# A graph layer with layer norm: first loads in another order, earlier statistics, degrees by one matmul

## The chip, the cores and the metric

The kernel runs on one core of a Trainium2 chip. The metric is device time in microseconds (us). Three runs of the kernel before took 436.0, 438.15 and 438.83 us, median 438.15.

## The reference

`x` is 4096x256 and `adj` 4096x4096, both float32. With N = 4096 rows:

```
h    = relu((x - mean) / sqrt(var + 1e-5))           # per row of x
deg  = sum(adj, axis=1) + 1e-5                       # per row of adj
out  = x + relu((adj / deg) @ h @ Wn.T + bn + h @ Ws.T + bs)
```

## The kernel before, in words

The host lays `adj` out so that a *unit* is a tile of 128 partitions x 2 x 512: two blocks of 128 columns of `adj` (the contraction) against the 512 rows of one of Q = 8 *groups*. A group has U = 16 units, so there are S = 128 units, and the list `order` (lines 33 and 34) interleaves groups 0 and 1 in the first 32 units, while h is still being made; from unit 32 on the groups follow each other. Unit s of group q and index u needs the two row tiles 2u and 2u+1 of h, called *pair* u. There are 16 pairs.

Products are in three terms of a rounded type: every operand is split into a high part (rounded, made by ScalarE) and a low part (the rest, made by VectorE), and hi*hi, hi*lo and lo*hi are added up in PSUM. A unit is therefore, in this order: a load into one of RING = 4 buffers `adj_raw` (SP's queue), `adj_hi` (ScalarE, line 292), `adj_lo` (VectorE, line 434), an addition into `total` for the degrees (VectorE, line 446; the first of a group is a copy, line 443) and 12 matmuls (TensorE, lines 573 to 575). For 14 units of the groups 0 and 1 the addition is instead a second load that adds in memory (`by_dma`, issued by GpSimd, line 239). The load of unit s waits until high part, low part and VectorE's addition of unit s - 4 are done; `adj_hi` and `adj_lo` of unit s wait until TensorE has used unit s - 4.

A pair of h is made by: a load of x (SP), statistics and their aggregation (VectorE, lines 397 and 401), rstd and shift (GpSimd, lines 214 to 225, started at `norm_at[p]`), two activations into `h_row` (ScalarE, line 295, at `make_at[p]`), `h_hi` (ScalarE, line 316, at `split_at[p]`) and `h_lo` (VectorE, line 426). Tiles 0 and 1 go a shorter way, with VectorE scaling (line 410) and the first unit cut into two halves (lines 312, 421, 555).

Each engine runs its own list in order: a loop over s with fixed places for the other work, so whatever waits holds what stands behind it. The lists at lines 45 to 56 are these places, counted in units. After its 16 units a group has: its product split (lines 351 and 469, at `product_at`), its h made again, transposed (line 590) and multiplied with Ws, then weighed with Wn (line 599), joined, activated, added to x and stored.

Degrees: when a group's units are in `total`, VectorE adds its two halves to `sums` (128x512, partition by row; line 458). TensorE then multiplies each of four 128x128 blocks of `sums` with a column of ones (line 623), which puts the degree of 128 rows into one column of a PSUM bank, and VectorE adds 1e-5 and takes the reciprocal (lines 474 and 476). The last group's degrees come directly ahead of unit 127. `weigh_last` and lines 533 to 538 are the tail of the last group: of its four tiles, 0 and 1 go through ScalarE and GpSimd (lines 387 and 283), 2 and 3 through VectorE (line 538).

Of the kernel before, what the change touches and what calls it, by code (L numbers as in the profile page):

```python
# [5 lines left out]
P = 128  # L6
# [9 lines left out]
RING = 4  # L16
# [5 lines left out]
def gnn_layer(nc, x, adj, wn, ws, bn, bs, out):  # L22
# [27 lines left out]
    product_at = [32, 42, 52] + [last_unit[q] + 3 for q in range(3, Q)]  # L50

    norm_at = [0, 0, 2, 3] + [2 * p - 4 for p in range(4, PAIRS)]

    make_at = [0, 1, 3] + [2 * p - 2 for p in range(3, PAIRS - 1)] + [2 * PAIRS - 5]
    split_at = [0, 1, 3] + [2 * p - 1 for p in range(3, PAIRS - 1)] + [2 * PAIRS - 4]
    sums_at = [38, 45, 54, 64] + last_unit[4:]

    with ExitStack() as ctx:
# [24 lines left out]
        ones = sb("ones", [P, 1])  # L83
# [8 lines left out]
        deg = sb("deg", [P, 2, UI])  # L92
# [17 lines left out]
        s_ones = sem("ones_ready")  # L110
# [50 lines left out]
        def _(sp):  # L161
# [19 lines left out]
            sp.dma_start(adj_raw[:, 0, 0, :], adj[0, 0, :, 0, :]).then_inc(s_raw0, 16)  # L181
            sp.dma_start(adj_raw[:, 0, 1, :], adj[0, 0, :, 1, :]).then_inc(s_raw[0], 16)
# [5 lines left out]
            for s in range(RING, S):  # L188
                load_unit(s)
                if s % 2 == 0 and s // 2 + 2 < PAIRS:  # L190
                    load_x(s // 2 + 2)
# [17 lines left out]
        def _(pool):  # L209
# [32 lines left out]

            def add_bias(q):
                pool.wait_ge(s_owned, q + 1)
                if q == 0:
                    pool.wait_ge(s_bsum, 1)
                nc.gpsimd.tensor_tensor(own[:, :, :], own[:, :, :], b_sum[:, :, :].broadcast_to([P, UI, F]), ALU.add) \  # L247
                  .then_inc(s_ownb, 1)
# [17 lines left out]
            nc.gpsimd.memset(ones[:, :], 1.0).then_inc(s_ones, 1)  # L266
            for s in range(S):
                for p in range(1, PAIRS):
                    if s == norm_at[p]:
                        norm(p)  # L270
                for n in range(len(by_dma)):
# [8 lines left out]
            for t in range(2):  # L280
                row = (Q - 1) * UI + t
                pool.wait_ge(s_relu, Q + t)
                nc.gpsimd.tensor_tensor(x_sb[:, row, :], x_sb[:, row, :], own[:, t, :], ALU.add).then_inc(s_tail[t], 1)

        @block.scalar
        def _(act):
# [70 lines left out]
            nc.scalar.dma_start(x_sb[:, 1, :], x[:, 1, :]).then_inc(s_x1, 16)  # L357
            nc.scalar.dma_start(x_sb[:, 2:4, :], x[:, 2:4, :]).then_inc(s_x[1], 16)
# [26 lines left out]
            for t in range(2):  # L385
                act.wait_ge(s_last, t + 1)
                nc.scalar.activation(own[:, t, :], own[:, t, :], ACT.Relu).then_inc(s_relu, 1)
# [6 lines left out]
        def _(dve):  # L394
# [54 lines left out]
            def join_sums(q):  # L449
                dve.wait_ge(s_add, vector_added[last_unit[q]])  # L450
                if q < 2:
# [3 lines left out]
                    dve.wait_ge(s_both, q + 1)  # L455
                if q >= 1:
                    dve.wait_ge(s_summed, q)
                nc.vector.tensor_tensor(sums[:, :], total[:, q % 3, 0, :], total[:, q % 3, 1, :], ALU.add).then_inc(s_sums, 1)
# [41 lines left out]
            split_unit(1)  # L500
            for s in range(2, S):
# [3 lines left out]
                for p in range(2, PAIRS):  # L505
# [29 lines left out]
            for t in range(2, UI):  # L535
# [6 lines left out]
        def _(pe):  # L542
# [37 lines left out]
            def turn(q):  # L580
# [5 lines left out]
                if q >= 1:  # L586
                    pe.wait_ge(s_deg, q)
# [26 lines left out]
            def sum_degrees(q):  # L614

                pe.wait_ge(s_sums, q + 1)
                pe.wait_ge(s_htlo, 2 * q + 2)
                if q == 0:
                    pe.wait_ge(s_ones, 1)
                else:  # L620
                    pe.wait_ge(s_deg, q)
                for t in range(UI):
# [76 lines left out]
```

## Time and profile before

| | |
|---|---|
| median of 3 runs | 438.15 us |
| the profiled execution | 436.03 us, span 434.0 us |
| TensorE | 419.2 us busy, 97% of the span, granted clock 0.995 on average |
| VectorE | 360.0 us, 83% |
| ScalarE | 208.0 us, 48% |
| GpSimd | 113.7 us, 26% |
| DMA | 83.98 MB, 194 GB/s on average |

Busy time of TensorE counts matmuls from start to a modelled end, and they overlap: a 512-column matmul is given 0.39 us, while the next one starts after 0.23. So its busy share says little about lost time; the starts do. In the timeline a row gives start, duration, engine, line, operation, out<-in, shape and count; in square brackets stands the idle time ahead of it and what ended that. PE is TensorE, DVE VectorE, ACT ScalarE, POOL GpSimd, SP SyncE; a q behind the name is the engine's issuing queue.

### The profile page before, as it was taken

The page shows a single profiled execution, that of the slowest core. Times are in us where ns is not written, and L with a number is a line of the kernel's source. Part 1 is how long each engine was busy: PE and PEld are TensorE (multiplying, and loading weights), DVE is VectorE, ACT ScalarE, POOL GpSimd, SP SyncE. Part 2 cuts the span into 40 slices and gives each one's busy share as a digit, 9 for nine tenths or more (in the row PEclk, how much of TensorE's full clock was granted, in tenths as well). Part 3 has the DMA queues.
Part 4 walks back from the last instruction along what each step waited for, and adds up shares of the span by engine and source line. Part 5 has one row for each costly group of instructions (what it writes and reads, how often), then busy time and mean ns, then how long its engine had stood idle before and what let it go on. Part 6 is the DMA issues. An engine that isn't in the chain of part 4 may idle for free.

```text
span 434.0 us, 5622 instructions
## 1 busy us (share of the span) xinstructions
PE 419.2 (97%) x2057; PEld 350.7 (81%) x2057; DVE 360.0 (83%) x421; ACT 208.0 (48%) x267; POOL 113.7 (26%) x107
## 2 busy tenths in 40 slices
PE   7799999988999999999999999999999999999995
PEld 4578877766888888888888888888888888888884
DVE  5688888989899896996797796979878897869934
ACT  4675555556533733734442544435342643426411
POOL 4365676741020303432203202002110302003021
PEclk9989999999999999999999999999999999999999
DMA  8779999999945474465347364545745465453501
GB/s 281 250 236 316 310 308 287 290 233 287 272 152 195 145 231 158 142 225 166 109 136 239 127 209 154 192 145 160 242 141 194 138 205 183 146 194 101 189 2 48
DMA packets 25482, 83.98 MB, mean 194 GB/s; under 512 B 2800, under 2 KB 4336, under 8 KB 25456
## 3 DMA queue, kind: packets, MB, share of 16 engines
q1 hardware_dynamic: 22864, 75.64, 52.0%
q0 software_dynamic: 2016, 7.34, 8.3%
q10 hardware_dynamic: 576, 0.66, 0.5%
q8 instruction: 16, 0.26, 0.3%
q14 instruction: 10, 0.08, 0.1%
HBM read 79.43 MB, written 4.19 MB: 193 GB/s over the span
## 4 chain that ended last, share of the span: by engine, by line
PE 74%; DVE 8%; POOL 8%; ACT 4%; issue 3%; DMA 3%; DVEq 0%; POOLq 0%; ACTq 0%; SPq 0%
PE banks L573 20%; PE banks L574 20%; PE banks L575 20%; PE banks L599 10%; DVE adj_lo L434 3%; POOL rstd L216 3%; POOL shift L225 2%; ACT adj_hi L292 2%; DMA adj_raw<-adj_in 2%; POOL rstd L214 2%; DVE total L446 2%; PE banks L590 2%; PE banks L623 1%; ACT h_row L295 1%; DVE stats L397 1%
## 5 line engine op out<-in xcount | busy, mean ns | idle before, releaser
L573 PE MATMUL banks<-adj_hi,h_hi 128*128 128x512 f32 x508 | 201.5, 397 | 7.6 <-DVE adj_lo L434 6.0
L292 ACT ACTIVATE adj_hi<-adj_raw 128x1024 fp32r<-128x1024 f32 x127 | 133.9, 1057 | 146.9 <-PE banks L575 128.2
L575 PE MATMUL banks<-adj_lo,h_hi 128*128 128x512 f32 x508 | 198.6, 391 | 0.0
L574 PE MATMUL banks<-adj_hi,h_lo 128*128 128x512 f32 x508 | 198.6, 391 | 0.0
L434 DVE TENSOR_TENSOR adj_lo<-adj_raw,adj_hi 128x1024 fp32r<-128x1024 f32 x127 | 167.4, 1318 | 35.4 <-ACT adj_hi L292 34.9
L446 DVE TENSOR_TENSOR total<-total,adj_raw 128x1024 f32<-128x1024 f32 x106 | 131.1, 1237 | 0.0
L573 PEld LDWEIGHTS banks<-adj_hi,h_hi 128*128 128x128 f32 x508 | 95.8, 189 | 31.5 <-issue 10.5
L575 PEld LDWEIGHTS banks<-adj_lo,h_hi 128*128 128x128 f32 x508 | 95.7, 188 | 20.6
L574 PEld LDWEIGHTS banks<-adj_hi,h_lo 128*128 128x128 f32 x508 | 95.9, 189 | 18.4
L253 POOL TENSOR_TENSOR x_sb<-x_sb,own 128x1024 f32<-128x1024 f32 x7 | 29.1, 4161 | 135.3 <-ACT own L355 135.3
L247 POOL TENSOR_TENSOR own<-own,b_sum 128x1024 f32<-128x1024 f32 x8 | 22.6, 2823 | 116.8 <-ACT own L340 116.8
L295 ACT ACTIVATE h_row<-x_sb,shift,rstd 128x256 f32<-128x256 f32 x62 | 32.9, 591 | 32.0 <-POOL shift L222 32.0
L474 DVE TENSOR_SCALAR deg<-banks 128x4 f32<-128x4 f32 x8 | 1.3, 162 | 22.0 <-PE banks L623 22.0
L351 ACT ACTIVATE p_hi<-banks 128x512 fp32r<-128x512 f32 x16 | 9.2, 597 | 20.3 <-PE banks L575 14.1
L599 PE MATMUL banks<-w_hi,ht_lo 128*128 128x256 f32 x64 | 18.1, 283 | 0.0
L599 PE MATMUL banks<-w_lo,ht_hi 128*128 128x256 f32 x64 | 18.1, 283 | 0.0
L599 PE MATMUL banks<-w_hi,ht_hi 128*128 128x256 f32 x64 | 18.1, 282 | 0.0
L216 POOL TENSOR_TENSOR rstd<-rstd,consts 128x2 f32<-128x2 f32 (+1 forms) x17 | 17.3, 1017 | 1.3
L214 POOL TENSOR_TENSOR rstd<-mv,consts 128x2 f32<-128x2 f32 (+1 forms) x17 | 10.5, 617 | 27.2 <-DVE mv L401 27.2
L239 POOL DMA_DIRECT2D total_dma<-adj_in x12 | 10.7, 891 | 22.0 <-PE banks L575 17.7
L599 PE MATMUL banks<-w_hi,p_lo 128*128 128x256 f32 x56 | 15.8, 283 | 0.0
L599 PE MATMUL banks<-w_lo,p_hi 128*128 128x256 f32 x56 | 15.8, 283 | 0.0
(65 smaller groups left out, 288.0 us busy)
## 6 DMA issues: line engine op xcount, KB each, us to landing
adj_raw<-adj_in SPq DMA_DIRECT2D x127, 512.0 KB, 4.0
total_dma<-adj_in POOLq DMA_DIRECT2D x14, 512.0 KB, 7.9
x_sb<-x_in SPq DMA_DIRECT2D x14, 256.0 KB, 6.0
rows_out<-x_sb SPq DMA_DIRECT2D x7, 512.0 KB, 5.0
adj_raw<-adj_in SPq DMA_DIRECT2D x2, 256.0 KB, 4.5
x_sb<-x_in ACTq DMA_DIRECT2D x1, 256.0 KB, 4.2
w_raw<-w_neigh SPq DMA_DIRECT2D x1, 256.0 KB, 5.4
w_raw<-w_self SPq DMA_DIRECT2D x1, 256.0 KB, 6.1
```

What stands on the lines that cost most here:

```text
L214: nc.gpsimd.tensor_tensor(rstd[:, cols], mv[:, cols, 1], consts[:, 0, 0:n], ALU.add).then_inc(s_rstd, 1)
L216: nc.gpsimd.tensor_tensor(rstd[:, cols], rstd[:, cols], consts[:, 1, 0:n], ALU.pow).then_inc(s_rstd, 1)
L247: nc.gpsimd.tensor_tensor(own[:, :, :], own[:, :, :], b_sum[:, :, :].broadcast_to([P, UI, F]), ALU.add) \
L253: nc.gpsimd.tensor_tensor(x_sb[:, rows, :], x_sb[:, rows, :], own[:, :, :], ALU.add).then_inc(s_final, 1)
L292: nc.scalar.activation(adj_hi[:, r, :, :], adj_raw[:, r, :, :], ACT.Copy).then_inc(s_hi, 1)
L295: return nc.scalar.activation(slot, x_sb[:, t, :], ACT.Relu, bias=shift[:, t:t + 1], scale=rstd[:, t:t + 1])
L434: nc.vector.tensor_tensor(adj_lo[:, r, :, :], adj_raw[:, r, :, :], adj_hi[:, r, :, :].bitcast(F32), ALU.subtract).then_inc(s_lo, 1)
L446: nc.vector.tensor_tensor(total[:, q % 3, :, :], total[:, q % 3, :, :], adj_raw[:, s % RING, :, :], ALU.add).then_inc(s_add, 1)
L573: nc.tensor.matmul(bank, h_hi[:, j, feats], adj_hi[:, r, a, :], start=first, stop=False)
L574: nc.tensor.matmul(bank, h_lo[:, j, feats], adj_hi[:, r, a, :], start=False, stop=False)
L575: done = nc.tensor.matmul(bank, h_hi[:, j, feats], adj_lo[:, r, a, :], start=False, stop=last)
L599: last = nc.tensor.matmul(bank, m[:, k, cols], w[:, k, which, :], start=(n == 0), stop=(n == len(terms) - 1))
```

## The change

Loads: all first loads go out on SP, in the order x tile 0, first half of unit 0, x tile 1, x pair 1, second half of unit 0, then as before; x pairs 4 and 5 follow unit 4, and later pairs come one pair earlier. VectorE's start is reordered, and it splits unit 2 ahead of pair 1's h_lo; ScalarE splits unit 2 ahead of making pair 1. The statistics of pairs 4 and up and their scale and shift come one unit earlier. Product 0 is split one unit earlier. Degrees: `sums` is transposed in blocks of 32x32 and each stretch of 32 is added up, which leaves 128x16 partial sums; one matmul with a 0/1 matrix `fold` (1 where two partitions are equal modulo 32) adds the four stretches of 32 partitions; VectorE picks each row's column with a mask and adds. `fold` is made by GpSimd at unit 30. Of the last group's tiles, tile 1 goes through VectorE as 2 and 3 do.

```diff
-    product_at = [32, 42, 52] + ...
+    product_at = [31, 42, 52] + ...
-    norm_at = [0, 0, 2, 3] + [2 * p - 4 for p in range(4, PAIRS)]
+    norm_at = [0, 0, 1, 2] + [2 * p - 5 for p in range(4, PAIRS)]
-    make_at = [0, 1, 3] + ...
-    split_at = [0, 1, 3] + ...
+    make_at = [0, 2, 3] + ...
+    split_at = [0, 2, 3] + ...
...
             sp.dma_start(x_sb[:, 0, :], x[:, 0, :]).then_inc(s_x[0], 16)
             sp.dma_start(adj_raw[:, 0, 0, :], adj[0, 0, :, 0, :]).then_inc(s_raw0, 16)
+            sp.dma_start(x_sb[:, 1, :], x[:, 1, :]).then_inc(s_x1, 16)
+            load_x(1)
             sp.dma_start(adj_raw[:, 0, 1, :], adj[0, 0, :, 1, :]).then_inc(s_raw[0], 16)
...
                 load_unit(s)
-                if s % 2 == 0 and s // 2 + 2 < PAIRS:
-                    load_x(s // 2 + 2)
+                if s == RING:
+                    load_x(4)
+                    load_x(5)
+                if s > RING and s % 2 == 0 and s // 2 + 3 < PAIRS:
+                    load_x(s // 2 + 3)
...
+            def make_fold():
+                nc.gpsimd.memset(fold[:, :], 0.0).then_inc(s_fold, 1)
+                for n, d in enumerate(range(-96, 128, 32)):
+                    pool.wait_ge(s_fold, n + 1)
+                    nc.gpsimd.affine_select(out=fold[:, :], in_=fold[:, :], compare_op=ALU.not_equal, fill=1.0,
+                                            base=d, pattern=[[-1, P]], channel_multiplier=1).then_inc(s_fold, 1)
...
-            nc.gpsimd.memset(ones[:, :], 1.0).then_inc(s_ones, 1)
...
+                if s == 30:
+                    make_fold()
...
-            nc.scalar.dma_start(x_sb[:, 1, :], x[:, 1, :]).then_inc(s_x1, 16)
-            nc.scalar.dma_start(x_sb[:, 2:4, :], x[:, 2:4, :]).then_inc(s_x[1], 16)
...
+                nc.vector.tensor_tensor(sums[:, :], total[:, q % 3, 0, :], total[:, q % 3, 1, :], ALU.add).then_inc(s_sums, 1)
+                dve.wait_ge(s_sums, q + 1)
+                nc.vector.transpose(total[:, q % 3, 0, :], sums[:, :]).then_inc(s_flipped, 1)
+                dve.wait_ge(s_flipped, q + 1)
                 if q >= 1:
                     dve.wait_ge(s_summed, q)
-                nc.vector.tensor_tensor(sums[:, :], total[:, q % 3, 0, :], total[:, q % 3, 1, :], ALU.add).then_inc(s_sums, 1)
+                nc.vector.tensor_reduce(part[:, :], total[:, q % 3, 0, :].rearrange("p (c s) -> p c s", s=32), AX.X, ALU.add) \
+                  .then_inc(s_part, 1)
...
             def degrees(q):
                 dve.wait_ge(s_summed, q + 1)
-                nc.vector.tensor_scalar(deg[:, 0, :], banks[:, SUMMED, 0:UI], DEG_EPS, None, ALU.add).then_inc(s_deg, 1)
-                dve.wait_ge(s_deg, q + 1)
+                if q == 0:
+                    dve.wait_ge(s_quarter, 5)
+                nc.vector.tensor_tensor(picked[:, :, :], banks[:, SUMMED, 0:R // 32].rearrange("p (t n) -> p t n", n=4),
+                                        in_quarter[:, :, :], ALU.mult).then_inc(s_deg, 1)
+                dve.wait_ge(s_deg, 3 * q + 1)
+                nc.vector.tensor_reduce(deg[:, 2, :], picked[:, :, :], AX.X, ALU.add).then_inc(s_deg, 1)
+                dve.wait_ge(s_deg, 3 * q + 2)
+                nc.vector.tensor_scalar(deg[:, 0, :], deg[:, 2, :], DEG_EPS, None, ALU.add).then_inc(s_deg, 1)
+                dve.wait_ge(s_deg, 3 * q + 3)
                 nc.vector.reciprocal(deg[:, 1, :], deg[:, 0, :]).then_inc(s_rdeg, 1)
...
+            nc.vector.memset(in_quarter[:, :, :], 0.0).then_inc(s_quarter, 1)
+            dve.wait_ge(s_quarter, 1)
+            for n in range(4):
+                nc.vector.memset(in_quarter[32 * n:32 * n + 32, :, n], 1.0).then_inc(s_quarter, 1)
             dve.wait_ge(s_x[0], 16)
             statistics((0,), 1)
+            first_scaled(0)
             dve.wait_ge(s_x1, 16)
             statistics((1,), 2)
-            first_scaled(0)
             first_half_unit(0)
-            first_scaled(1)
             first_low(0)
             pair_statistics(1)
+            first_scaled(1)
+            first_half_unit(1)
             first_low(1)
-            first_half_unit(1)
             split_unit(1)
-            for s in range(2, S):
+            pair_statistics(2)
+            split_unit(2)
+            split_h(1)
+            pair_statistics(3)
+            for s in range(3, S):
...
-                for p in range(2, PAIRS):
+                for p in range(4, PAIRS):
                     if s == norm_at[p]:
                         pair_statistics(p)
...
             def sum_degrees(q):
-                pe.wait_ge(s_sums, q + 1)
+                pe.wait_ge(s_part, q + 1)
                 pe.wait_ge(s_htlo, 2 * q + 2)
...
-                for t in range(UI):
-                    last = nc.tensor.matmul(banks[:, SUMMED, t:t + 1], sums[:, t * P:(t + 1) * P], ones[:, :],
-                                            start=True, stop=True)
-                last.then_inc(s_summed, 1)
+                nc.tensor.matmul(banks[:, SUMMED, 0:R // 32], fold[:, :], part[:, :], start=True, stop=True) \
+                  .then_inc(s_summed, 1)
```

## Rows read from the trace of the kernel before

**Rows 1.** Chain that ended last, shares of the span by engine.

```profile
PE 74%; DVE 8%; POOL 8%; ACT 4%; issue 3%; DMA 3%; DVEq 0%; POOLq 0%; ACTq 0%; SPq 0%
```

**Rows 2.** Busy time by stretch; then TensorE's granted clock, DMA share, GB/s.

```profile
core 0: us, PE busy (x) PEld busy (x) DVE busy (x) ACT busy (x) POOL busy (x), PEclk, DMA share, GB/s
8.00:12.00 4.00, 3.32 (x14) 2.15 (x13) 2.29 (x5) 2.25 (x4) 2.28 (x4) 1.00 1.04 409
24.00:28.00 4.00, 4.00 (x14) 3.20 (x13) 3.69 (x7) 1.31 (x3) 3.47 (x4) 0.68 0.79 236
54.00:107.00 53.00, 49.00 (x207) 37.59 (x206) 47.15 (x67) 31.27 (x46) 30.36 (x35) 1.00 1.01 283
285.50:336.70 51.20, 51.20 (x258) 43.52 (x257) 43.47 (x43) 23.05 (x27) 5.82 (x2) 1.00 0.52 174
```

**Rows 3.** Timeline of TensorE: first matmuls of units 1, 2, 4, 5, 15, 32.

```profile
10.50 0.47 PE L573 MATMUL banks<-adj_hi,h_hi 128*128 128x512 f32 x1 [0.19 <-DVE adj_lo L434]
...
14.89 0.47 PE L573 MATMUL banks<-adj_hi,h_hi 128*128 128x512 f32 x1 [1.43 <-DVE adj_lo L434]
...
22.53 0.47 PE L573 MATMUL banks<-adj_hi,h_hi 128*128 128x512 f32 x1 [1.95 <-DVE adj_lo L434]
...
26.95 0.40 PE L573 MATMUL banks<-adj_hi,h_hi 128*128 128x512 f32 x1
...
54.16 0.45 PE L573 MATMUL banks<-adj_hi,h_hi 128*128 128x512 f32 x1
...
106.73 0.50 PE L573 MATMUL banks<-adj_hi,h_hi 128*128 128x512 f32 x1 [1.60 <-DVE p_lo L469]
```

**Rows 4.** Timeline of all engines, the first 13 us.

```profile
1.65 0.42 SPq L182 DMA_DIRECT2D adj_raw<-adj_in  x1
...
5.54 0.41 DVE L410 TENSOR_SCALAR h_row<-x_sb,mv,rstd 128x256 f32<-128x256 f32 x1 [0.50 <-POOL rstd L216]
...
6.70 0.64 ACT L312 ACTIVATE adj_hi<-adj_raw 128x512 fp32r<-128x512 f32 x1 [0.29 <-DMA adj_raw<-adj_in]
...
7.13 0.75 DVE L397 BATCH_NORM_STATS2 stats<-x_sb 128x6 f32<-128x256 f32 x2
7.23 0.29 POOL L264 TENSOR_SCALAR_AFFINE_SELECT ident<-ident 128x128 f32<-128x128 f32 x1
7.24 0.41 ACT L308 ACTIVATE h_hi<-h_row 128x256 fp32r<-128x256 f32 x1
...
7.91 0.25 DVE L401 BATCH_NORM_AGGREGATE mv<-stats 128x2 f32<-128x6 f32 x2
...
8.04 1.06 ACT L292 ACTIVATE adj_hi<-adj_raw 128x1024 fp32r<-128x1024 f32 x1 [0.39 <-DMA adj_raw<-adj_in]
...
9.13 1.23 DVE L434 TENSOR_TENSOR adj_lo<-adj_raw,adj_hi 128x1024 fp32r<-128x1024 f32 x1
...
10.78 1.09 ACT L295 ACTIVATE h_row<-x_sb,shift,rstd 128x256 f32<-128x256 f32 x2 [1.69 <-POOL shift L222]
...
11.91 0.63 ACT L316 ACTIVATE h_hi<-h_row 128x512 fp32r<-128x512 f32 x1
...
12.57 0.69 DVE L426 TENSOR_TENSOR h_lo<-h_row,h_hi 128x512 fp32r<-128x512 f32 x1 [2.22 <-ACT h_hi L316]
```

**Rows 5.** All waits of ScalarE from 54 to 94 us: total, times, longest.

```profile
ACT h_row L295 <- POOL shift L222: 15.5, 7, 3.5
```

**Rows 6.** Timeline of TensorE: one degree sum and the next unit's first matmul.

```profile
285.64 0.94 PE L623 MATMUL banks<-ones,sums 128*128 128x1 f32 x8
286.44 0.49 PE L573 MATMUL banks<-adj_hi,h_hi 128*128 128x512 f32 x1
```

**Rows 7.** DMA queues, 54 to 94 us: packets, MB, share of 16 engines.

```profile
q1 hardware_dynamic: 2640, 8.29, 59.1%
q0 software_dynamic: 864, 3.15, 41.4%
```

**Rows 8.** Timeline of VectorE: its first operation on the last group's degrees.

```profile
423.66 0.16 DVE L474 TENSOR_SCALAR deg<-banks 128x4 f32<-128x4 f32 x1 [7.60 <-PE banks L623]
```

More of the change, by code:

```diff
@@ L48, in gnn_layer @@
     degrees_at = [w + 1 for w in weigh_at[:-1]]
-    product_at = [32, 42, 52] + [last_unit[q] + 3 for q in range(3, Q)]
-    norm_at = [0, 0, 2, 3] + [2 * p - 4 for p in range(4, PAIRS)]
-    make_at = [0, 1, 3] + [2 * p - 2 for p in range(3, PAIRS - 1)] + [2 * PAIRS - 5]
-    split_at = [0, 1, 3] + [2 * p - 1 for p in range(3, PAIRS - 1)] + [2 * PAIRS - 4]
+    product_at = [31, 42, 52] + [last_unit[q] + 3 for q in range(3, Q)]
+    norm_at = [0, 0, 1, 2] + [2 * p - 5 for p in range(4, PAIRS)]
+    make_at = [0, 2, 3] + [2 * p - 2 for p in range(3, PAIRS - 1)] + [2 * PAIRS - 5]
+    split_at = [0, 2, 3] + [2 * p - 1 for p in range(3, PAIRS - 1)] + [2 * PAIRS - 4]
     sums_at = [38, 45, 54, 64] + last_unit[4:]
@@ L82, in gnn_layer @@
         sums = sb("sums", [P, R])
-        ones = sb("ones", [P, 1])
+        fold = sb("fold", [P, P])
+        in_quarter = sb("in_quarter", [P, UI, 4])
+        part = sb("part", [P, R // 32])
+        picked = sb("picked", [P, UI, 4])
         ident = sb("ident", [P, P])
@@ L91, in gnn_layer @@
         consts = sb("consts", [P, 3, 2])
-        deg = sb("deg", [P, 2, UI])
+        deg = sb("deg", [P, 3, UI])
         banks = ctx.enter_context(nc.psum_tensor("banks", [P, 8, 512], F32))
@@ L109, in gnn_layer @@
         s_ident = sem("ident_ready")
-        s_ones = sem("ones_ready")
+        s_fold = sem("fold_step_done")
+        s_quarter = sem("in_quarter_ready")
+        s_flipped = sem("sums_flipped")
+        s_part = sem("part_sums_ready")
         s_consts = sem("consts_ready")
@@ L279, in _ @@
             add_bias(Q - 1)
[L280 to L283, printed above, removed]
+            row = (Q - 1) * UI
+            pool.wait_ge(s_relu, Q)
+            nc.gpsimd.tensor_tensor(x_sb[:, row, :], x_sb[:, row, :], own[:, 0, :], ALU.add).then_inc(s_tail[0], 1)
         @block.scalar
@@ L384, in _ @@
             product_high(Q - 1)
-            for t in range(2):
-                act.wait_ge(s_last, t + 1)
-                nc.scalar.activation(own[:, t, :], own[:, t, :], ACT.Relu).then_inc(s_relu, 1)
+            act.wait_ge(s_last, 1)
+            nc.scalar.activation(own[:, 0, :], own[:, 0, :], ACT.Relu).then_inc(s_relu, 1)
             for b in range(2, UI):
@@ L534, in _ @@
                                                in1=own[:, t, :], op0=ALU.mult, op1=ALU.add).then_inc(s_last, 1)
-            for t in range(2, UI):
+            for t in range(1, UI):
                 row = (Q - 1) * UI + t
@@ L586, in turn @@
                 if q >= 1:
-                    pe.wait_ge(s_deg, q)
+                    pe.wait_ge(s_deg, 3 * q)
                 for k in range(KC):
@@ L614, in sum_degrees @@
             def sum_degrees(q):
-                pe.wait_ge(s_sums, q + 1)
+                pe.wait_ge(s_part, q + 1)
                 pe.wait_ge(s_htlo, 2 * q + 2)
                 if q == 0:
-                    pe.wait_ge(s_ones, 1)
+                    pe.wait_ge(s_fold, 8)
                 else:
-                    pe.wait_ge(s_deg, q)
-                for t in range(UI):
-                    last = nc.tensor.matmul(banks[:, SUMMED, t:t + 1], sums[:, t * P:(t + 1) * P], ones[:, :],
-                                            start=True, stop=True)
-                last.then_inc(s_summed, 1)
+                    pe.wait_ge(s_deg, 3 * q)
+                nc.tensor.matmul(banks[:, SUMMED, 0:R // 32], fold[:, :], part[:, :], start=True, stop=True) \
+                  .then_inc(s_summed, 1)
             def weigh(q):
```

## The prediction, made before the change was run

> **What bounds it now.** I read the chain of waits first: 74% of it is TensorE [rows 1], so the question is when TensorE is not fed. Busy time doesn't say, because the ends of matmuls are modelled; the starts of the units do (a unit is 12 matmuls of 512 columns). From unit 5 to unit 15 a unit takes (54.16 - 26.95)/10 = 2.72 us [rows 3]; that is TensorE's own pace. Unit 1 to unit 5 takes 16.45 us where four units need 10.88, and unit 15 to unit 32 takes 52.57 where 17 need 46.25. So 5.6 us are lost at the start and 6.3 us between units 15 and 32. In the stretch of a later group of rows TensorE is busy for all of its 51.20 us [rows 2], and a microsecond there can only be won by taking work off TensorE.
>
> Of the 5.6 us, 1.7 are a clock loss: unit 4 runs from 22.53 to 26.95, 4.42 us, and the granted clock of 24 to 28 us is 0.68 on average, so part of it at the lower of the two levels (1.2 of 2.4 GHz), behind a gap of 1.95 us [rows 2, 3]. The rest are gaps on adj_lo of units 2 and 4. In the first rows VectorE waits 2.22 us for h_hi before it goes on to unit 2, and ScalarE waited 1.69 us for the shift before it made that h [rows 4]: an in-order queue stands behind a chain of statistics. Most of the 6.3 us has the same cause: all of ScalarE's waits between 54 and 94 us, 15.5 us in 7, are for GpSimd's shift, none is for a load [rows 5].
>
> **The change, part by part.** *First loads.* Tile 1 and pair 1 go from ScalarE's queue to SP's, two issues of some 0.42 us [rows 4], so everything behind them on SP is issued up to 0.9 us later. The second half of unit 0 is taken on landing at 6.70 and unit 1 at 8.04 [rows 4]; in the order below they are needed at 9.0 and 9.45, so I cost the delay at nothing. ScalarE loses two issues ahead of a wait; nothing comes of that either. Five small memsets on VectorE lie ahead of its first load.
>
> *The start, walked through.* VectorE scales tile 0 until 5.95 as before. The statistics of tile 1 now come behind that (one of the pair's, 0.4 + 0.2), so the low half of unit 0 ends near 7.3, h_lo near 7.6, then pair 1's statistics (7.13 to 8.16 before, 1.03) end at 8.6, tile 1 is scaled by 9.0 (0.41), ScalarE's h_hi of it is there at 9.45 (0.41) and only then does ScalarE split unit 1, until 10.5 (1.06); VectorE's part ends at 11.75 (1.23). TensorE starts unit 1 at 11.8, **1.3 us later** than 10.50 [rows 3, 4]. From there the new order pays. ScalarE splits unit 2 by 11.55 without waiting for h; the shift of pair 1 is there at 8.6 + 2.6 = 11.2 (8.16 to 10.78 before), h is made by 12.65 and h_hi by 13.3 (1.09, 0.63). VectorE: pair 2's statistics to 12.7, unit 2 to 13.9, h_lo to 14.5 (0.69). Unit 2 starts at 14.55 and no longer at 14.89. Then pair 3's statistics to 15.5, unit 3 to 16.7 (TensorE wants it at 17.3), pair 4's to 17.7, the copy to 18.3, h_lo to 19.0, unit 4 to 20.2; ScalarE waits for shift 2 until 12.7 + 2.6 = 15.3 and has unit 4 split at 18.1. Unit 4 starts at 20.2, 2.3 us earlier. With no gap ahead of it that is longer than 0.3 us I take full clock: another 1.7. **Unit 5 starts 4.0 us earlier, at 22.9.** Bounds: 5.6, all that is lost there now, and 0.
>
> *Statistics with more lead.* From pair 4 on they move one unit ahead, and the x loads of SP with them (one pair ahead, no new wait in front). That is 2.7 us more for GpSimd's chain. ScalarE's 15.5 us in 7 waits are 2.2 each, so they vanish but for the longest. What is late next? VectorE: four units cost it six operations of 128x1024 (four splits, two additions) at the split's 1.23, two h_lo of 0.69 and two statistics of 1.03, 10.8 by these rows where TensorE needs 10.88; the measured busy share between 54 and 107 us, 47.15 of 53, is 9.7 per 10.88 [rows 2, 4]. It keeps ahead, narrowly. Low part of product 0 one unit earlier: unit 32 waited 1.60 us for it [rows 3]; now it stands behind unit 31 on ScalarE and VectorE, whose queues wait for TensorE to finish unit 29, two units before unit 32, and p_hi and the split of unit 32 need 0.63 + 1.06 + 1.23 = 2.9 us after that, by the rows of that size [rows 4]: covered by 5.4. So units 15 to 32 go at 2.72 and **6.3 us** are won; unit 32 starts at 96.4, not 106.73, 10.3 us earlier. Bounds: 6.3 and, if only another wait takes the place, 0.
>
> *Degrees.* Now each group of rows issues 4 matmuls, 8 records, in 0.80 us between its first and the next unit's [rows 6]. One matmul of 16 columns is 2 records of the same weights, 0.2 us at the same 0.1 each; at most 0.46, twice the 0.23 of a 512-column matmul. 0.6 saved (0.34 at least) eight times, seven of them and the last in dense TensorE time: **4.8 us** (2.7 to 4.8). In exchange VectorE gets, per group, a transpose and a reduction of 128x512 and two operations on 128x16. No row shows them. Nearest is h_lo, 128x512 from two operands, at 0.69 [rows 4]; bounds 0.34 (half of it) and, for the farthest row, twice the split of 1024 elements, 2.5. I take 0.69 each and 0.2 for each small one (one of 128x4 took 0.16 [rows 8]), 1.8 in all. In a group of 51.2 us VectorE is busy for 43.5 [rows 2], so 7.7 are free; and behind the last sums it waited 7.60 us for TensorE's matmul [rows 8]. Cost on the path nothing; were that cover gone, 1.8 eight times, 14 us.
> The Trainium skill speaks against the reduction (VectorE: DVE Perf Modes, Rules for kernel authors: tensor_reduce only runs in the slowest mode and should be kept off a hot path). By that rule too the sum is unchanged as long as VectorE isn't the bound; no row here shows a reduction.
>
> *Rest.* The fold matrix is eight GpSimd operations in place of one memset; one such select took 0.29 [rows 4]; I allow up to five times that, 2 to 11 us, once, at a point where GpSimd has only additions by DMA behind it, which are needed 20 us later. The last tile 1 goes from ScalarE and GpSimd to VectorE, one operation of 128x256 (0.41 as [rows 4] have such) ahead of tiles 2 and 3: 0, between -0.4 and +0.5.
>
> **Sum.** 4.0 + 6.3 + 4.8 = 15.1 us. The profiled execution was 436.03, so it would be 420.9; the median of the runs, 438.15, stands 2.1 above it, which gives **423**.
>
> **Rivals.** *The ring of loads becomes the bound (3 in 10).* The DMA engines' share is 1.01 from 54 to 107 us [rows 2]. From 54 to 94 SP's queue took 59.1% of 40 us for 8.29 MB, 2.85 us per MB, and the adding queue 41.4% for 3.15 MB, 5.26 per MB [rows 7]. Four units are 2.62 MB of units and x and, at one added by DMA per 2.5 units, 0.84 of additions: 11.9 us, 2.97 a unit, where TensorE wants 2.72. If these are real occupancy, units 12 to 32 go from 42.0 to 101.4, less a lead of 2: 7.3 + 4.8 won, **426**; if the old pace of units 15 to 32 stays outright, 4.0 + 4.8 won, **429.3**. For it speaks the share; against it, that ScalarE waits for no load there [rows 5] and that 8 to 12 us shows 409 GB/s at a share of 1.04 [rows 2], so a share near one isn't a ceiling of bytes.
> The Trainium skill (DMA: Bandwidth & Descriptors, Where 436 GB/s comes from) puts the HBM side of a core at some 358 GB/s. Four units need 3.46 MB in 10.88 us, 318 GB/s, which that rule allows, and by it alone this rival would have 1 in 10; the 409 measured here is above its figure.
>
> *The clock falls in the new first gaps (1 in 10).* TensorE now idles for over 1 us ahead of the second half of unit 0 and ahead of unit 1. If one or two units then run as unit 4 does now, 1.7 to 3.4 us are lost again, 2.5 in the middle: **425.5**. Against it: there were gaps there before, at full clock.
>
> *The degrees don't get cheaper (1 in 20)*, because the matmul of 128x16 costs as much as the four: **427.8**.
>
> *Slower: VectorE becomes the bound of every group (3 in 100).* Place: the sums ahead of each degree matmul. Price: beyond 7.7 us of added VectorE time in a group, TensorE waits for the excess, eight times. To end 4.4 us above 438 it takes 10.3 + 4.4 of excess, 1.8 a group, so a transpose and a reduction of over 4.5 us each, nearly seven times the row taken: **443** and more.
>
> **Numbers.** My forecast has 5 in 10, 419.5 to 425 by its own bounds. Range 419.5 to 429.5: the low end is the sum with a start that wins all of 5.6 and the runs near the profiled execution, the high end is the ring at its old pace. About 1% is what a measurement of this kernel can tell from no change, 433.8 to 442.5. Faster than that: forecast, ring, clock and degrees, 0.88; same 0.08, two of the rivals together; slower 0.04.
>
> **What would show it.** Unit 1 starting near 11.8, unit 2 near 14.5, unit 4 near 20 at full clock; no wait of ScalarE for the shift beyond 1 us after pair 4; unit 32 near 96 to 97; two records per degree matmul and 0.2 us; VectorE idle still above 5 us per group. I am wrong if ScalarE's waits turn to waits for adj_raw between 30 and 95 us, if the granted clock drops below 1 between 8 and 20 us, or if TensorE waits on the partial sums.

## The result, and the profile after

The changed kernel takes **430.67 us** (median) beside 438.1 for the kernel before: a ratio of 0.9848, 95% interval 0.981 to 0.9886. The gain is 1.5%, about half of what I forecast. One of the four runs of the changed kernel took 2355.36 us; it is left out of the ratio, and why it was so long is not known. The profiled execution is 430.28 us with a span of 428.5; before it was 436.03 and 434.0, so 5.5 us of span have to be placed.

The rows of after, in the order of the rows of before. First TensorE's timeline, at the first matmuls of units 1, 2, 4, 5, 15, 32 [rows 3] and, new, of unit 46 (start, duration, engine and line, operation; in brackets the idle time ahead and what ended it):

```profile
11.88 0.77 PE L610 MATMUL banks<-adj_hi,h_hi 128*128 128x512 f32 x1
...
15.20 0.39 PE L610 MATMUL banks<-adj_hi,h_hi 128*128 128x512 f32 x1
...
20.66 0.47 PE L610 MATMUL banks<-adj_hi,h_hi 128*128 128x512 f32 x1
...
23.48 0.39 PE L610 MATMUL banks<-adj_hi,h_hi 128*128 128x512 f32 x1
...
53.70 0.58 PE L610 MATMUL banks<-adj_hi,h_hi 128*128 128x512 f32 x1 [2.86 <-DVE adj_lo L450]
...
104.90 0.47 PE L610 MATMUL banks<-adj_hi,h_hi 128*128 128x512 f32 x1 [0.47 <-DVE adj_lo L450]
...
152.79 0.50 PE L610 MATMUL banks<-adj_hi,h_hi 128*128 128x512 f32 x1 [1.57 <-DVE adj_lo L450]
```

Unit 5 starts 3.47 us earlier than before. At unit 15 almost all of that is gone (53.70 for 54.16): TensorE stood 2.86 us in front of it, at a place where it had not waited before. By unit 32 the lead is 1.83. From unit 5 to unit 32 TensorE takes 81.42 us where 79.78 were needed before; units 5 to 15 lose 3.0 of these, units 15 to 32 win 1.4 (51.20 for 52.57).

The same starts for every kernel of this study, in us, from TensorE's timeline of each (27 units at 2.72 would be 73.4 from unit 5 to 32). The medians were not all taken side by side: the kernel before took 438.1 us beside after and 435.8 to 436.0 beside the others, so whole kernels are to be compared by their ratios to before:

| kernel | unit 5 | unit 5 to 32 | unit 32 to 127 | unit 45 to 46 | span | median |
|---|---|---|---|---|---|---|
| before | 26.95 | 79.78 | 316.76 | 2.72 | 434.0 | 438.1 |
| after | 23.48 | 81.42 | 313.06 | 4.45 | 428.5 | 430.67 |
| after, no adding loads | 22.27 | 73.44 | 310.99 | 2.72 | 417.2 | 419.41 |
| after, adding loads made plain | 23.65 | 74.65 | 312.02 | 3.59 | 420.8 | 422.09 |
| after, statistics at old places | 23.31 | 80.50 | 313.19 | 4.43 | 427.5 | 428.85 |
| before, no adding loads | 25.44 | 80.36 | 316.81 | 2.72 | 433.1 | 435.24 |
| before, degrees part alone | 27.24 | 78.78 | 312.53 | 3.78 | 429.0 | 431.13 |
| after, w and b earlier | 23.45 | 77.25 | 314.04 | 4.44 | 425.2 | 426.71 |
| after, x in fours | 22.80 | 81.26 | 312.86 | 4.13 | 427.4 | 428.36 |
| after, fold later | 23.42 | 81.64 | 312.69 | 3.97 | 428.3 | 429.7 |
| after, three fixes | 23.16 | 76.85 | 311.30 | 2.72 | 421.8 | 425.11 |
| three fixes, sparser adding | 22.73 | 75.04 | 312.29 | 2.72 | 420.5 | 422.59 |
| the same, x in fours | 23.38 | 75.82 | 311.69 | 2.72 | 421.4 | 423.9 |
| sparser adding, old places | 23.40 | 81.33 | 311.67 | 2.72 | 426.9 | 428.81 |

Behind unit 127 all of them take 10.5 us. Kernels with the new start differ by 1.4 us at unit 5 and those with the old one by 1.8, which is the scatter of that figure.

Next the windows of after, against [rows 2]: the first stretch of the start, the end of the start, units 15 to 32, one late group from degree matmul to degree matmul, and the 2 us behind the new gap (busy time and count of each engine, granted clock, DMA share, GB/s):

```profile
core 0: us, PE busy (x) PEld busy (x) DVE busy (x) ACT busy (x) POOL busy (x), PEclk, DMA share, GB/s
8.00:12.00 4.00, 2.73 (x7) 1.72 (x7) 2.55 (x5) 3.28 (x5) 0.83 (x3) 0.69 1.03 401
24.00:28.00 4.00, 4.00 (x19) 3.31 (x18) 3.97 (x7) 3.51 (x6) 3.41 (x6) 1.00 1.03 324
54.00:107.00 53.00, 50.88 (x213) 40.52 (x212) 48.46 (x67) 32.73 (x46) 34.79 (x41) 0.97 0.93 256
283.10:333.55 50.45, 50.45 (x254) 42.84 (x252) 44.83 (x47) 22.94 (x27) 8.32 (x2) 1.00 0.53 179
54.00:56.00 2.00, 2.00 (x6) 1.53 (x5) 1.97 (x5) 2.00 (x4) 1.34 (x2) 0.50 0.30 119
```

The clock loss of 24 to 28 us is gone, but there are two new ones: from 8 to 12 us the granted clock is 0.69 on average, behind the 1.82 us for which TensorE waited ahead of the second half of unit 0, and from 54 to 56 it is 0.50, which is the 1.2 GHz level, behind the gap at unit 15. Unit 15 takes 4.41 us for that and not 2.72. The late group is 50.45 us long where it was 51.20.

ScalarE's waits, 54 to 94 us [rows 5] and then 24 to 108 (line waited for: total, times, longest):

```profile
ACT adj_hi L311 <- DMA adj_raw<-adj_in: 10.8, 7, 3.1
ACT h_row L314 <- POOL shift L233: 3.4, 3, 1.7
```

```profile
ACT adj_hi L311 <- DMA adj_raw<-adj_in: 29.0, 15, 4.0
ACT h_row L314 <- POOL shift L233: 3.8, 4, 1.7
```

The kernel before shows for 24 to 108 us:

```profile
ACT h_row L295 <- POOL shift L222: 26.3, 10, 4.6
ACT adj_hi L292 <- DMA adj_raw<-adj_in: 7.8, 4, 3.1
```

The two lines have changed places. The waits for the shift are nearly gone, as forecast (26.3 us became 3.8), and nearly as many microseconds of waits for the next unit's load stand where they were. The chain of waits of after names the same thing ahead of unit 15 (start, duration, what):

```profile
38.72 12.51 DMA adj_raw<-adj_in
...
51.25 1.06 ACT adj_hi L311
...
52.33 1.22 DVE adj_lo L450
```

It is a load of 512 KB that took 12.51 us to land. Of after's three unit loads issued between 38 and 44 us the trace gives the first row, of before's two between 38 and 46 the second (shortest, median, longest):

```profile
DMA to landing us min/median/max: 10.6/11.3/12.5
```

```profile
DMA to landing us min/median/max: 7.2/7.4/7.6
```

With four buffers in the ring a load has 4 x 2.72 = 10.9 us, less the two splits of the unit that must leave the buffer (1.06 and 1.23): by this estimate what takes over some 8.6 us comes late, or 7.4 where VectorE also adds that unit (1.22). The two queues, 54 to 94 us [rows 7]:

```profile
q1 hardware_dynamic: 2321, 7.55, 54.1%
q0 software_dynamic: 711, 2.61, 34.6%
```

The degrees: one sum and the next unit's first matmul [rows 6], VectorE's first operation on the last degrees [rows 8], and VectorE's work ahead of unit 46's split:

```profile
282.95 0.29 PE L659 MATMUL banks<-part,fold 128*128 128x16 f32 x2
283.08 0.48 PE L610 MATMUL banks<-adj_hi,h_hi 128*128 128x512 f32 x1
```

```profile
418.15 0.17 DVE L498 TENSOR_TENSOR picked<-banks,in_quarter 128x16 f32<-128x16 f32 x1 [5.25 <-PE banks L659]
```

```profile
148.20 1.21 DVE L469 TENSOR_TENSOR total<-total,total_dma 128x1024 f32<-128x1024 f32 x1
149.44 0.69 DVE L472 TENSOR_TENSOR sums<-total 128x512 f32<-128x512 f32 x1
150.17 0.71 DVE L475 STREAM_TRANSPOSE total<-sums 128x512 f32<-128x512 f32 x1
150.92 0.69 DVE L479 TENSOR_REDUCE part<-total 128x16 f32<-128x512 f32 x1
151.52 1.22 DVE L450 TENSOR_TENSOR adj_lo<-adj_raw,adj_hi 128x1024 fp32r<-128x1024 f32 x1
```

The next unit now starts 0.13 us behind the degree matmul, not 0.80. The transpose and the reduction stand in VectorE's queue straight ahead of adj_lo of unit 46, and unit 46 comes 1.7 us late. How late depends on VectorE's lead, the time from the start of unit 45's split on VectorE to its first matmul: the lead is 2.8 us here, 3.4 in before with the degrees part alone, 3.6 with plain loads and 4.5 without adding loads, and unit 46 is 1.73, 1.06, 0.87 and 0 late, each time what the lead lacks of 4.5.

The chain's shares against [rows 1]; DMA has gone from 3% to 8%:

```profile
PE 71%; DVE 12%; DMA 8%; ACT 3%; issue 2%; POOL 2%; SPq 1%; DVEq 0%; ACTq 0%; POOLq 0%
```

**Where the 5.5 us come from.** Start +3.47, units 5 to 32 -1.64, eight degree sums +5.4 (0.66 to 0.68 each), units 46 and 47 -1.9: together 5.3, the rest is scattered. The start's part is not firm: of before's loss there, 1.7 us are the clock loss at unit 4, and the kernel before without its adding loads, whose start is the same, has none in its trace (granted clock 1.00 from 24 to 28 us behind a gap of 1.66) and starts unit 5 at 25.44, not 26.95.

### The profile page after: what moved, and what is told of

Its sections match the earlier page's. It is cut to its first block, busy times and chain, and to the rows that moved or that the text cites. A ratio compares the mean times of both kernels' runs of the same rounds, so it can differ in the third digit from the quotient of the medians.

```text
span 428.5 us, 5577 instructions
## 1 busy us (share of the span) xinstructions
PE 414.2 (97%) x2009; PEld 347.0 (81%) x2009; DVE 377.5 (88%) x459; ACT 207.6 (48%) x266; POOL 128.8 (30%) x113
## 4 chain that ended last, share of the span: by engine, by line
PE 71%; DVE 12%; DMA 8%; ACT 3%; issue 2%; POOL 2%; SPq 1%; DVEq 0%; ACTq 0%; POOLq 0%
PE banks L610 20%; PE banks L611 20%; PE banks L612 20%; PE banks L636 10%; DMA adj_raw<-adj_in 8%; DVE adj_lo L450 5%; DVE total L462 3%; ACT adj_hi L311 2%; PE banks L627 1%; DVE stats L413 1%; ACT h_row L314 1%; POOL rstd L227 1%; POOL shift L233 1%; PE banks L678 0%; DVE p_lo L491 0%
## 5 line engine op out<-in xcount | busy, mean ns | idle before, releaser
L272 POOL TENSOR_TENSOR x_sb<-x_sb,own 128x1024 f32<-128x1024 f32 x7 | 30.6, 4375 | 127.5 <-ACT own L374 127.5
L266 POOL TENSOR_TENSOR own<-own,b_sum 128x1024 f32<-128x1024 f32 x8 | 31.7, 3961 | 111.2 <-ACT own L359 111.2
L227 POOL TENSOR_TENSOR rstd<-rstd,consts 128x2 f32<-128x2 f32 (+1 forms) x17 | 18.4, 1080 | 1.3
L636 PE MATMUL banks<-w_hi,p_hi 128*128 128x256 f32 x56 | 15.8, 282 | 0.0
```

Source lines behind the costliest of these rows:

```text
L227: nc.gpsimd.tensor_tensor(rstd[:, cols], rstd[:, cols], consts[:, 1, 0:n], ALU.pow).then_inc(s_rstd, 1)
L272: nc.gpsimd.tensor_tensor(x_sb[:, rows, :], x_sb[:, rows, :], own[:, :, :], ALU.add).then_inc(s_final, 1)
L636: last = nc.tensor.matmul(bank, m[:, k, cols], w[:, k, which, :], start=(n == 0), stop=(n == len(terms) - 1))
```

## Experiments

My theory after the result: the loads that add into `total_dma` hold up the unit loads of SP's queue until the ring is empty, and this was hidden before because TensorE was already waiting for late statistics. Rivals: the bytes alone are too many; the x loads with small packets are at fault; the earlier statistics are of no use here; VectorE's added work is the bound.

### Is it the adding loads, and is it their bytes or the adding?

**No adding loads** (the 12 units that they add are missing from the degrees; the first two loads, which only store, stay):

```diff
-                    pool.dma_start(total_dma[:, q, :, :], adj[q, u, :, :, :], accum_op=ALU.add).then_inc(s_dadd[q], 16)
+                    (for n >= 2: nothing)
```

> The changed kernel without the 12 loads that add in memory (units of groups 0 and 1 are then missing from their degrees). Theory A, the adding loads slow SP's queue until the ring of loads runs dry: no gap at unit 15, unit 5 to unit 32 in 73.4 to 75 us instead of 81.4, ScalarE's waits for adj_raw between 24 and 108 us under 5 us instead of 28.9, the whole some 7 us faster than the changed kernel, 423 to 424. Theory B, the statistics between split and addition of every fourth unit hold the loads back: nothing of that changes, the gap at unit 15 stays, 430 to 431. Theory C, the small loads of w and b at units 9 to 13 fill the queue: the gap at unit 15 shrinks to about half, the rest up to unit 32 stays, 428 to 429.

Measured: 419.41 us, ratio 0.9629 (0.9593 to 0.9664). From unit 5 to 32 TensorE takes 73.44, its own pace to the hundredth. ScalarE from 24 to 108 us now waits mostly for TensorE to free a buffer:

```profile
ACT adj_hi L309 <- PE banks L610: 15.6, 14, 1.7
ACT adj_hi L309 <- DMA adj_raw<-adj_in: 7.0, 4, 2.1
```

By the spans the adding loads cost the changed kernel 11.3 us, by the ratios 9.5. 8.0 of them lie between units 5 and 32 and 2.1 behind unit 32, as unit 46 isn't late either; the other 1.2 lie ahead of unit 5, where no adding load has been issued (the first goes out at 37.29 in after), and are scatter.

**The same loads, plain** (each only stores; same bytes, same points of issue; each replaces what was there, so the degrees lack the units loaded ahead of it):

```diff
-  pool.dma_start(total_dma[...], adj[q, u, ...], accum_op=ALU.add)
+  pool.dma_start(total_dma[...], adj[q, u, ...])
```

> The changed kernel with the 12 adding loads turned into plain loads of the same bytes over the same tile, at the same places (the sums of groups 0 and 1 are then those of one unit). If the adding is what slows SP's queue (it needs a read of the destination and a write), the loads land in 5 to 7 us instead of 8 to 10, the gap at unit 15 is gone and unit 5 to 32 takes 75 to 77 us: some 5 us faster than the changed kernel. If it is only the bytes, nothing changes: the gap at unit 15 stays and 81 us.

Measured: 422.09 us, ratio 0.9687 (0.9662 to 0.9711), 74.65 from unit 5 to 32. The DMA issues from 54 to 94 us, first of this kernel, then of after (form, count, KB, median us to landing):

```profile
adj_raw<-adj_in SPq DMA_DIRECT2D x15, 512.0 KB, 5.8
total_dma<-adj_in POOLq DMA_DIRECT2D x8, 512.0 KB, 6.3
```

```profile
adj_raw<-adj_in SPq DMA_DIRECT2D x14, 512.0 KB, 7.8
total_dma<-adj_in POOLq DMA_DIRECT2D x6, 512.0 KB, 8.5
```

With the same bytes all landings are 2 us shorter, and 6.8 of the 8.0 us come back between units 5 and 32. So it is the adding, and only 1.2 the bytes. What in the adding slows the other loads was not tried. The Trainium skill (DMA: Bandwidth & Descriptors, Where 436 GB/s comes from) has some 358 GB/s of the HBM side bind such loads. The traces don't show that as the limit here: with the additions the queues are full at less (from 36 to 54 us the share is 1.02 at 305 GB/s), and 8 to 12 us goes above it at 401 [rows 2 had 409].

### What are the earlier statistics worth?

**After, statistics and x loads at their old places:**

```diff
-    norm_at = [0, 0, 1, 2] + [2 * p - 5 for p in range(4, PAIRS)]
+    norm_at = [0, 0, 1, 2] + [2 * p - 4 for p in range(4, PAIRS)]
...
-                if s == RING: load_x(4); load_x(5)
-                if s > RING and s % 2 == 0 and s // 2 + 3 < PAIRS: load_x(s // 2 + 3)
+                if s % 2 == 0 and s // 2 + 2 < PAIRS: load_x(s // 2 + 2)
```

> The changed kernel with the statistics from pair 4 on and the x loads back at the places of before; start and degrees stay changed. Theory A: loads still late between 35 and 50 us, the gap at unit 15 stays within 1 us, unit 5 to 32 at 80 to 82 us, total 430 to 431. Theory B: the gap at unit 15 goes, ScalarE waits for the shift again, 15 us between 54 and 94, unit 5 to 32 at 79 to 80, total 427 to 428.

Measured: 428.85 us, ratio 0.9846 (0.9823 to 0.987), so no slower than after. ScalarE's two lines (24 to 108 us) change places once more, and the gap at unit 15 is gone although the adding loads, w and b are where they were:

```profile
ACT h_row L311 <- POOL shift L230: 24.0, 9, 4.6
ACT adj_hi L308 <- DMA adj_raw<-adj_in: 9.9, 4, 4.5
```

In this kernel the step that I had priced at 6.3 us is worth nothing or a little less.

**Before, without its adding loads** (the same 12 units missing):

> The kernel before without its 12 adding loads (the first two, which only store, stay; those 12 units are missing from the degrees). Question: how much of what the kernel before loses between units 15 and 32 (6.3 us) came from the late statistics, which was the reason given in the prediction, and how much from the adding loads. Theory (statistics: all of ScalarE's waits there were for GpSimd's shift): units 15 to 32 still take 51 us or more, the kernel 434 to 436. Rival (the adding loads also slow the x loads on which the statistics stand, and those unit loads that nobody was seen to wait for): units 15 to 32 take 46.3 to 48 us and the kernel 429 to 432.

Measured: 435.24 us, ratio 0.9969 (0.9943 to 0.9995). Units 15 to 32 take 51.9 us, and ScalarE still waits for the shift, 26.4 us in 7 from 24 to 108 us:

```profile
ACT h_row L293 <- POOL shift L222: 26.4, 7, 4.6
ACT adj_hi L290 <- DMA adj_raw<-adj_in: 5.3, 5, 1.9
```

So my reading of the kernel before was right: its loss there came from the statistics. Without the additions it gains 0.7 us (1.4 by the ratio); in after the same edit gains 9.5 by the ratio. And yet the additions slow the loads here too: the unit loads issued from 54 to 94 us landed in a median of 5.8 us with them and 3.3 without. They were hidden behind the late statistics.

**Sparser adding loads, statistics at old places** (the best kernel, told below, with the edit of the first experiment of this group):

> The kernel with the three fixes and sparser adding loads, with the statistics and x loads from pair 4 on back at the places of before. Where the loads no longer run dry, this is what the earlier statistics are worth. Theory (the prediction's step: late shifts cost TensorE time): units 5 to 32 take 4 us longer than with the early ones, ScalarE again waits over 15 us for the shift, and the kernel takes 426 to 427. Rival (the shift was only late because the x loads came late on a queue that the adding loads held up): within 1 us of 422.6.

Measured: 428.81 us, ratio 0.9821 (0.9773 to 0.9868), by the medians 6.2 us more than the same kernel with early statistics (422.59), by the ratios 5.2. Units 5 to 32 take 81.33 for 75.04. 1.7 of these 6.3 us are a clock loss behind a late unit (unit 28 takes 4.39 us); ScalarE's waits:

```profile
ACT h_row L311 <- POOL shift L230: 28.5, 9, 4.6
...
ACT adj_hi L308 <- DMA adj_raw<-adj_in: 2.4, 2, 1.3
```

Put together, units 5 to 32 take 78.8 to 81.3 us if the statistics are late (before with and without the new degrees, and the three kernels of this group), and 81.42 if they are early and the additions and the loads of w and b as they were (after). Only with both mended do they take 73.4 to 75.8. Either cause alone keeps most of the loss; the second can be halved without touching the additions, as the loads of w and b show below (77.25).

### Is VectorE's added work free?

**Before, with the degrees part alone:** (the diff's `make_fold`, transpose, reduction, one matmul and the mask; nothing else)

> The kernel before with the new degrees alone. The changed kernel's units show 0.66 to 0.69 us saved by each of eight matmuls, 5.4 in all, and unit 46 coming 1.7 us late behind the second group's transpose and reduction. If that late unit belongs to the degrees, this kernel is 3.7 us faster than before, span 430.3; if it came from the changed kernel's poorer lead, the full 5.4, span 428.6.

Measured: 431.13 us, ratio 0.9904 (0.9877 to 0.9931). The degrees alone shorten the span by 5.0 us, 4.2 of them behind unit 32 (and 4.2 by the ratio), although unit 46 comes 1.06 late here as well. After, which has the start and the statistics as well, is at 0.9848 with an interval that overlaps: those two parts added little, 2.4 us by the ratios.

### What else makes the loads late?

**w and b loaded earlier.** In before and after alike, w_neigh, w_self and the two biases (768 KB) go out behind units 9, 11 and 13, in after from 22.9 to 33.2 us. They stand ahead of the 12.51 us load in the queue; when that was issued, at 38.72, the last bias was still under way (it landed at 42.96):

```diff
-                if s == 9:    (w_neigh)    if s == 11:   (w_self)    if s == 13:   (biases)
+                if s == 6:    (w_neigh)    if s == 7:    (w_self)    if s == 7:    (biases)
```

> The changed kernel with the loads of w and b moved from behind units 9, 11 and 13 to behind units 6 and 7, ahead of the adding loads. Theory C: no gap at unit 15, no clock drop there, 4.7 us faster than the changed kernel, 425 to 426. Theory A: the backlog builds a little later, the gap moves behind unit 16 or shrinks by at most 1.5 us, 429 to 431. Theory B: the same as the changed kernel.

Measured: 426.71 us, ratio 0.979 (0.9761 to 0.982). The gap at unit 15 and the clock loss behind it are gone, and units 5 to 32 take 77.25, 4.2 less. What is left are late units around 23: ScalarE still waits 30.2 us for loads from 24 to 108 us. By the ratios the whole kernel gains 2.5 us on after, with intervals that touch; unit 44 comes 1.1 us late here, as in no other kernel.

**x in fours of tiles** (one load of 4 KB packets for two of 2 KB):

```diff
-                if s == RING: load_x(4); load_x(5)
-                if s > RING and s % 2 == 0 and s // 2 + 3 < PAIRS: load_x(s // 2 + 3)
+                if s == RING or s % 4 == 2 and s // 2 + 3 < PAIRS:
+                    p = 4 if s == RING else s // 2 + 3
+                    sp.dma_start(x_sb[:, 2 * p:2 * p + 4, :], x[:, 2 * p:2 * p + 4, :])
```

> The changed kernel with x from pair 4 on loaded in fours of tiles, 4 KB to a partition instead of 2 KB, half as many packets. If beside an adding load SP's queue gets on packet by packet, whatever their size, x costs half: the gap at unit 15 shrinks from 3.0 to 0 to 1 us and unit 5 to 32 to 77 to 79 us, 2 to 4 us faster than the changed kernel. If bytes count, x costs the same: within 1 us of it.

Measured: 428.36 us, ratio 0.983 (0.9808 to 0.9853); units 5 to 32 take 81.26, as in after. The gap at unit 15 shrinks by 1.0 and comes back later. The size of the packets isn't the cause.

**The fold matrix at unit 38, not 30.** GpSimd makes it from 89.5 to 98.7 us in after, and the additions behind it go out in a pair:

```profile
88.34 1.81 POOL L250 DMA_DIRECT2D total_dma<-adj_in  x2
89.50 0.86 POOL L256 MEMSET fold<- 128x128 f32 x1
90.52 8.22 POOL L259 TENSOR_SCALAR_AFFINE_SELECT fold<-fold 128x128 f32<-128x128 f32 x7
98.69 0.88 POOL L250 DMA_DIRECT2D total_dma<-adj_in  x1
100.02 0.87 POOL L250 DMA_DIRECT2D total_dma<-adj_in  x1 [0.46 <-issue]
```

> The changed kernel with the fold matrix made at unit 38, behind the last adding load, instead of at unit 30. It took GpSimd 9.2 us in which two adding loads queued up and then went out 1.3 us apart. If that pair is what makes units 31 and 32 late (0.8 us each), they come 0.5 to 1.5 us earlier and the total is as much faster; if their loads are late for the DMA rate alone, less than 0.5 us changes. The gap at unit 15 stays either way.

Measured: 429.7 us, ratio 0.9865 (0.9832 to 0.9899); 81.64 from unit 5 to 32. It costs nothing where it is.

### Towards a better version

**Three fixes at once:** w and b earlier, fold at unit 38, and group 1's sums two units later:

```diff
-    sums_at = [38, 45, 54, 64] + last_unit[4:]
+    sums_at = [38, 47, 54, 64] + last_unit[4:]
```

> The changed kernel with three repairs: loads of w and b behind units 6 and 7, the fold matrix at unit 38, and the second group's sums at unit 47 instead of 45. The first gave 2.1 us on its trace and took away the gap at unit 15; the third should take away the 1.7 us ahead of unit 46. Adding loads still in place, so waits for adj_raw stay: unit 5 to 32 in 76 to 77 us, total 1.5 to 3 us faster than with w and b alone, span 422 to 424.

Measured: 425.11 us, ratio 0.9771 (0.974 to 0.9801). Unit 46 starts 2.72 behind unit 45: a transpose and a reduction that come two units later are covered. Units 23 and 24 are still late (3.88 and 3.79).

**The same with sparser adding loads,** and that with x in fours:

```diff
-    by_dma = [(0, 0), (1, 0)] + [(1 - u % 2, u) for u in range(1, U - 3)]
+    by_dma = [(0, 0), (1, 0)] + [(1 - u % 2, u) for u in range(1, U - 5)]
...
-                pool.wait_ge(s_used, 5 * n // 2 + 2)
+                pool.wait_ge(s_used, 3 * n + 2)
...
-                    if s == 5 * n // 2 + 5:
+                    if s == 3 * n + 5:
```

> The three fixes together, and in addition the loads that add are one in three units in place of two in five, and two fewer of them (12 in all, ten of them adding); VectorE adds those two units itself. Units 5 to 32 take 76.85 us with the three fixes and 73.4 where nothing is late. Theory (each adding load holds up the loads of SP's queue, so what counts is how many run per unit): the stall around units 22 to 24 goes, units 5 to 32 take 74 to 75, the kernel 422.5 to 424. Rival (VectorE, at 1.23 us per addition, is the next to be late when it gets two more): units 5 to 32 stay at 76 to 78, TensorE waits for adj_lo, 425 or more.

> As the kernel with sparser adding loads, and x from pair 4 on comes in fours of tiles, each packet 4 KB in place of 2 KB. If small packets still cost SP's queue something once the additions are sparse, 1 us less than its neighbour; if what the queue lacks is only the adding loads, the same within 0.7 us; if the larger x loads stand in front of a unit load at a bad moment, 1 us more.

Measured: **422.59 us** (ratio 0.9702, 0.9676 to 0.9729) and 423.9 (0.9719, 0.9698 to 0.974). Of the first, every unit from 6 to 30 starts 2.72 behind the one before it. Fours gain nothing here either. What is left stands at units 31 and 32 (3.58 and 3.46 behind their predecessors) and at unit 55 (3.40). The chain of waits ahead of unit 31 names a load again, for which ScalarE stood 5.14 us:

```profile
82.68 9.14 DMA adj_raw<-adj_in
...
91.84 1.07 ACT adj_hi L311
...
92.93 1.01 DVE adj_lo L450
```

Behind it unit 32 has p_lo ahead of its adj_lo on VectorE. At unit 55 one adj_lo, behind group 2's sums, took 2.68 us where the others took 1.22; an addition of 128x1024 on GpSimd ran beside it (172.63 to 175.04 us). ScalarE's waits for loads are hardly shorter in this kernel than in after (29.0), from 24 to 108 us:

```profile
ACT adj_hi L311 <- DMA adj_raw<-adj_in: 26.3, 17, 5.1
```

So neither these waits nor a full share (1.00 at 289 GB/s from 54 to 98 us here) is by itself a loss. They cost time where the load's lateness passes through both splits and reaches TensorE, as at units 15 and 31. The first kernel of the two is faster than both kernels of this case; as its edits were chosen on these runs, its 422.6 is the best measured and not a limit.

## Why the prediction was wrong, step by step

**The step that failed** is "So units 15 to 32 go at 2.72 and 6.3 us are won". Its first half held: ScalarE's waits for the shift fell from 15.5 us to 3.4. The second half, "What is late next?", was answered with VectorE alone, and it was the loads. Units 15 to 32 gave +1.4 us and not +6.3, and units 5 to 15, which had gone at TensorE's own pace, lost 3.0, so -1.6 in all. One of the prediction's own signs of being wrong came: waits of ScalarE for adj_raw, 10.8 us from 54 to 94. That the step itself was sized about right is shown where the loads are mended: early statistics are worth 5 to 6 us there, 1.7 of them a clock loss, and without adding loads units 5 to 32 go at exactly 2.72, 73.44 us for 80.36 in the kernel before without its adding loads.

**Where the reading went astray.** I held against the ring of loads that ScalarE waits for no load from 54 to 94 us [rows 5]. This row could not speak on that: each late shift gave the loads time, so their lateness could not be seen. Its window was narrow, too: from 24 to 108 us ScalarE did wait for loads, 7.8 us in 4. The row that could was the DMA share of 1.01 at 283 GB/s [rows 2], and I set it aside because another stretch had a share of 1.04 at 409. Those 409 were plain loads only. That the additions were what brought it down I had in [rows 7], 5.26 us per MB against 2.85, and gave it 3 in 10.

**The rival that came.** Its pace of 2.97 a unit, worked out from [rows 7], agrees with 81.42 / 27 = 3.02 for units 5 to 32, but in part by luck: 4.7 us of these are the one gap at unit 15 and the slow unit behind it, and the others went at 2.84. With w and b earlier it is 77.25 / 27 = 2.86. The loads cost time in bursts and not as a steady pace. Its time of 426 was too low for two reasons that it didn't hold: unit 32 came at 104.90 and not at 101.4, by the gap and the clock loss at unit 15 (with w and b earlier it comes at 100.70), and units 46 and 47 lost 1.9 us. 426 + 3.5 + 1.9, less 0.6 for the better degrees, is 430.8. The upper end of the range, 429.5, had the ring but not unit 46.

**The second step that failed** is that VectorE's extra work costs "on the path nothing". Its size was right (0.71 and 0.69 for 0.69 each, and two more small ones of 0.17 for 0.2 each), and so is the average (44.83 of 50.45 busy, 5.25 us idle behind the last sums). But cover isn't an average. Group 1's sums stand at unit 45 in front of a split that TensorE needs next, in a stretch where VectorE has little lead (2.8 us), and there 1.9 us were lost (1.2 with the degrees alone). With a lead of 4.5, without adding loads, nothing was lost at the same place, and two units later nothing either. The Trainium skill (VectorE: DVE Perf Modes, Rules for kernel authors) would keep tensor_reduce off a hot path; the reduction took 0.69 us, as long as the addition of the same 128x512 ahead of it, and its place and not its pace was what cost.

**What held.** The walk through the start: unit 1 at 11.88 (11.8 forecast), unit 4 at 20.66 (20.2), unit 5 at 23.48 (22.9), 3.5 us won for 4.0 (2.0 against the one trace of the old start that has no clock loss). I said that I would be wrong if the granted clock dropped between 8 and 20 us, and it did, from about 9 to 13: unit 2 started at 15.20 and not at 14.55. The ten other kernels with this start show 1.00 from 8 to 12 us, so it comes with some executions only. As unit 4 had to wait for VectorE anyway, no more than 0.3 us were left of it there (the kernel with three fixes, without this loss, starts unit 4 at 20.32). The degrees: two records of a matmul, 0.7 us saved per group for 0.6. The fold matrix: 9.2 us of GpSimd, within the 2 to 11, at no cost. Waits of ScalarE for the shift did not all fall below 1 us, as I had it: the longest is 1.7.

## What to carry to other kernels

Before you book the gain of a wait that goes away, ask for each resource behind it how far it is ahead without that wait: an engine that waits for one thing shows no wait for another. A queue whose DMA share is already 1.0 is a candidate, though not a proof (the best kernel here has 1.00 too), and a share is to be priced by the kind of transfer in it, since a mix with loads that add filled it here at 283 to 305 GB/s where plain loads moved 401 to 409. Idle time in a group covers new work only where it lies ahead of the work's deadline, so look at what stands behind the new operations in the queue.

## What the runs showed of the hardware

- A 512 KB load that adds into its destination landed in a median of 8.5 us from 54 to 94 us, and made the plain loads beside it take 7.8; made plain itself, it landed in 6.3 and the others in 5.8; with none the others took 3.4 (kernel times 430.67, 422.09, 419.41). In the kernel before, with the same additions, the adding load took 7.8 and the plain ones 5.8, or 3.3 without additions.
- In after single loads took up to 12.51 us (a unit) and 12.97 (x, half as large), beside adding loads and shortly behind 768 KB of weights and biases; moving the latter ahead by three to six units took 4.2 us off units 5 to 32.
- Behind gaps of 1.82 and 2.86 us in after, and of 2.14 ahead of unit 28 in the kernel with sparser adding loads and old places, TensorE ran at the lower clock level for some 3 us each. Behind the gaps of 0.98 and 1.43 us that the kernel with w and b earlier has at the same point of the start it kept 1.00 (8 to 13 us), and so it did behind 1.66 in the kernel before without adding loads (24 to 28 us).
- GpSimd's select on 128x128 took 0.29 us for the identity at 7.2 us and 0.56 to 1.38 each, 8.22 for seven, beside a busy VectorE at 90 us. Why was not tried.
